# Expert rows padded to tiles of 128 slots instead of pairs of 256: 68 pairs, each half with its own expert

## The reference

```python
x = x + mamba2_layer(xn, ...) + moe(xn, router, gating, up, down)

def moe(x, router, gating, up, down):       # 8 experts, top 2, F = 256
    probs = softmax(x @ router)
    weights, indices = top_k(probs, 2)
    w = softmax(weights)
    fuse = silu(x @ gating[e]) * (x @ up[e])     # 128 -> 256, for each expert e of the token
    return sum over the two experts of w_e * (fuse @ down[e])   # 256 -> 128
```

## Time and profile before

| | |
|---|---|
| median of three runs | 825.52 us (822.66 to 828.09) |
| the profiled execution | 826.36 us, of which the span of the trace is 824.6 us |
| mean granted TensorE clock | 0.925 |
| router and top 2 | 0 to about 120 us |
| mamba2 layer | about 120 to 512 us |
| expert stage, first to last `gate_up` | 515.65 to 767.19 us |
| drain of the pipeline and last scatters | to about 783 us |
| sum and store | to 824.6 us |

### The profile page before, as it was taken

One profiled execution on the slowest core, in us unless ns is written; L12 is line 12 of the kernel. 1 busy time (PEld: TensorE's weight loads), 2 busy tenths in 40 slices (PEclk: granted clock), 3 DMA queues, 4 the chain that ended last, 5 costly groups with the idle time before them and its releaser, 6 DMA issues. The chain is left out here.

```text
span 824.6 us, 15776 instructions
## 1 busy us (share of the span) xinstructions
PE 649.1 (79%) x3781; PEld 546.2 (66%) x3783; DVE 608.1 (74%) x1486; ACT 469.9 (57%) x1030; POOL 455.4 (55%) x616
## 2 busy tenths in 40 slices
PE   0694638899889899988999897998888888889400
PEld 0694226787777787777778776787777777778300
DVE  7777999989989998999989996455555555546222
ACT  0441537678877877887767874345555555545200
POOL 3000017667777777777768785155555555555543
PEclk9999999989979998998989996899999999999855
DMA  9960100000000000000000043133323333333099
GB/s 303 260 139 0 28 1 25 23 25 25 25 21 20 28 21 24 25 25 24 21 21 28 24 133 92 40 98 95 87 87 91 95 91 91 88 93 93 10 272 338
DMA packets 72135, 62.52 MB, mean 76 GB/s; under 512 B 9544, under 2 KB 65231, under 8 KB 72112
## 3 DMA queue, kind: packets, MB, share of 16 engines
q1 hardware_dynamic: 63408, 45.19, 20.8%
q0 software_dynamic: 8704, 17.06, 6.0%
HBM read 30.73 MB, written 32.54 MB: 77 GB/s over the span
## 5 line engine op out<-in xcount | busy, mean ns | idle before, releaser
L442 POOL DMA_INDIRECT moe_d<-raw,slot_st x144 | 141.8, 984 | 131.9 <-issue 107.9
L416 POOL DMA_INDIRECT slots_d<-rows,slot_st x128 | 143.4, 1120 | 64.2 <-DVE xdt L1106 28.6
L1030 DVE SCALAR_TENSOR_TENSOR act<-raw,taps,act 128x512 f32<-128x512 f32 x192 | 163.2, 851 | 14.4 <-ACT act L511 11.1
L396 POOL TENSOR_TENSOR xde<-xdt,e_end 128x256 f32<-128x256 f32 x64 | 47.5, 742 | 113.2 <-DVE xdt L1106 111.5
L1223 DVE CAST x_hi<-bank 128x256 fp32r<-128x256 f32 x72 | 30.6, 425 | 104.4 <-PE bank L862 92.8
L855 PE MATMUL bank<-xw_hi,x_hi 128*128 x144 | 65.2, 453 | 30.5 <-DVE x_lo L1225 30.1
L881 PE MATMUL bank<-act,raw 128*128 x576 | 76.3, 276 | 0.7 <-issue 0.5
L662 ACT ACTIVATE raw<-bank 128x256 f32<-128x256 f32 x72 | 28.2, 392 | 85.4 <-remote 77.5
L772 PE MATMUL bank<-xdt,m_sb 128*128 128x64 f32 x512 | 74.1, 293 | 2.2 <-POOL xde L396 1.6
L772 PEld LDWEIGHTS bank<-xdt,m_sb 128*128 128x128 f32 x512 | 71.0, 211 | 4.3 <-issue 1.7
L881 PEld LDWEIGHTS bank<-act,raw 128*128 128x128 f32 x576 | 70.0, 192 | 1.5 <-issue 1.4
(11 more groups left out here) (234 smaller groups left out, 1727.0 us busy)
## 6 DMA issues: line engine op xcount, KB each, us to landing
slots_d<-rows SPq DMA_DIRECT2D x8, 1188.0 KB, 14.4
rows<-slots_d SPq DMA_DIRECT2D x72, 132.0 KB
act<-moe_d SPq DMA_DIRECT2D x12, 512.0 KB, 7.3
x_sb<-in_x SPq DMA_DIRECT2D x8, 512.0 KB, 6.6
act<-in_x SPq DMA_DIRECT2D x64, 64.0 KB
out<-x_sb SPq DMA_DIRECT2D x8, 512.0 KB, 7.2
moe_d<-raw,slot_st POOLq DMA_INDIRECT x144
slots_d<-rows,slot_st POOLq DMA_INDIRECT x128
```

Of the source, the lines that this page charges most:

```text
L396: nc.gpsimd.tensor_tensor(by_head(xde[:, u, :]), by_head(xdt[:, u, :]), per_head(e_end, nn), ALU.mult).then_inc(xde_done, 1)
L416: nc.gpsimd.indirect_dma_start(out=slots_d, out_offset=bass.IndirectOffsetOnAxis(ap=slot_st[:, r, c:c + 1], axis=0), in_=rows[:, r, c, :], ...
L442: nc.gpsimd.indirect_dma_start(out=moe_d, out_offset=bass.IndirectOffsetOnAxis(ap=slot_st[:, r, c:c + 1], axis=0), in_=ym[r][:, c * D:(c + ...
L1030: V.scalar_tensor_tensor(out=group_act(par)[:, t, :], in0=proj[:, t, k:k + GT], scalar=taps[:, t, k:k + 1], in1=group_act(par)[:, t, :], o ...
```

## The change

A tile of 128 slots (`TP` = 136 of them) takes the place of a pair as the unit of padding. An expert's slots begin at a multiple of 128. The pipeline still handles two tiles at a time, 68 pairs instead of 72, but the two halves of a pair can belong to different experts, so `eid` has an entry for each half and PE reads two entries in `gate_up` and two in `down`.

```diff
 PS = 2 * P
-MP = K * NT * P // PS + E
+TP = K * NT + E
+MP = TP // 2
...
-        eid = sb("eid", [1, MP], I32)
+        eid = sb("eid", [1, TP], I32)
...
-                    if not checked:
+                    if not isinstance(m, int) or TURN0 - 1 <= m < TURN1:
                         for fn in beside:
-                            fn(m - TURN0, r)
+                            fn(m - TURN0 + 1, r)
...
                 sp.dma_start(rows[:, r, :, :], slots_d[bass.ds((m * R + r) * PS, PS), :]
-                             .rearrange("(p c) v -> p c v", c=2)).then_inc(ld_slot[r], 16)
+                             .rearrange("(c p) v -> p c v", c=2)).then_inc(ld_slot[r], 16)
...
-            def expert(m, r):
-                return pe.value_load(eid[0:1, bass.ds(m * R + r, 1)], min_val=0, max_val=E - 1)
+            def expert(m, r, c):
+                return pe.value_load(eid[0:1, bass.ds((m * R + r) * 2 + c, 1)], min_val=0, max_val=E - 1)
 
             def gate_up(m, r):
-                ex = expert(m, r)
+                ex = [expert(m, r, c) for c in range(2)]
                 pe.wait_ge(xts_done, m * R + r + 1)
                 for c in range(2):
                     for a, (xs, w) in enumerate(((x_hi, gu_hi), (x_hi, gu_lo), (x_lo, gu_hi))):
                         gu = mm(bank[2 + 2 * (r % 2) + c][:, :], xs[:, r % 2, c * P:(c + 1) * P],
-                                w[:, bass.ds(ex * (2 * F), 2 * F)], start=(a == 0), stop=(a == 2))
+                                w[:, bass.ds(ex[c] * (2 * F), 2 * F)], start=(a == 0), stop=(a == 2))
...
             def down(m, r):
-                ex = expert(m, r)
+                ex = [expert(m, r, c) for c in range(2)]
...
-                               dn_sb[:, bass.ds(ex * (2 * D) + f * D, D)], start=(f == 0), stop=(f == 1))
+                               dn_sb[:, bass.ds(ex[c] * (2 * D) + f * D, D)], start=(f == 0), stop=(f == 1))
...
-            chain(V.tensor_scalar(cnt_i, incl[:, NT - 1, :], float(PS - 1), None, ALU.add))
-            chain(V.tensor_scalar(cnt_i, cnt_i, PS.bit_length() - 1, None, ALU.arith_shift_right))
+            chain(V.tensor_scalar(cnt_i, incl[:, NT - 1, :], float(P - 1), None, ALU.add))
+            chain(V.tensor_scalar(cnt_i, cnt_i, P.bit_length() - 1, None, ALU.arith_shift_right))
...
-            chain(V.tensor_scalar(base_s, base, float(PS), None, ALU.mult))
+            chain(V.tensor_scalar(base_s, base, float(P), None, ALU.mult))
```

More of the change, by code:

```diff
@@ L153, in program @@
         base_s = small[:, 928:936]
-        iota_r = small[:, 936:936 + MP].bitcast(I32)
-        iota_f = small[:, 1080:1080 + MP]
-        eid_f = small[:, 1220:1220 + MP]
+        iota_r = small[:, 936:936 + TP].bitcast(I32)
+        iota_f = small[:, 1080:1080 + TP]
+        eid_f = small[:, 1220:1220 + TP]
         tokid = small[:, 1360:1360 + NT].bitcast(I32)
@@ L236, in turn @@
                             fn(m + (r - lag) // R, (r - lag) % R)
-                    if not checked:
+                    if not isinstance(m, int) or TURN0 - 1 <= m < TURN1:
                         for fn in beside:
-                            fn(m - TURN0, r)
+                            fn(m - TURN0 + 1, r)
             lags = [lag for _, lag in stages]
-            assert (TURN1 - TURN0) * R == NT and 0 <= min(lags) and max(lags) <= R
+            assert (TURN1 - TURN0 + 1) * R == NT and 0 <= min(lags) and max(lags) <= R
             for m in range(TURN0):
@@ L383, in _ @@
             chain(pool.iota(rev_i, pattern=[[-1, E]], base=E, channel_multiplier=0))
-            chain(pool.iota(iota_r, pattern=[[1, MP]], base=0, channel_multiplier=0))
+            chain(pool.iota(iota_r, pattern=[[1, TP]], base=0, channel_multiplier=0))
             pool.wait_ge(consts, 1)
```

## The result

The changed kernel takes 869.2 us (median of six runs, 865.2 to 871.7), the kernel before 826.7 us on the same chip (median of six, 822.7 to 828.1). The ratio is 1.052, with an interval of 1.050 to 1.055: 5% slower. Another chip (D in the table of experiments) gave 865.2 against 826.8 us, 1.047 (1.043 to 1.051). The forecast was 873 us, slower.

What follows compares the result with a forecast made beforehand. PE's sequencer, nearly the bound in every second pair, was to become the bound at 4.45 us a pair: 826.4 + 46.7 + 1 = 874 us profiled, 873 us as median. The range was 842 to 902 us.

Steps and rivals of the forecast that it cites:

- The bound: Expert stage: PE's sequencer, ready after 2.75 us, is only 0.2 us from being the bound in every second pair.
- Two more reads at 0.75 us each: PE's sequencer, `gate_up` and `down`: two more reads of `eid` in each of 68 pairs add 1.5 us a pair.
- the late signal: PE's late signal to DVE in every second pair, now costing 1.15 us, costs nothing inside a 4.45 us pitch.
- Four offsets, 0.5 us: PE's sequencer: two more offsets each in `gate_up` and `down`, 0.5 us a pair together; lower bound nothing.
- The wait for `h_done` goes: In `turn_h`: the sequencer's wait of about 0.4 us vanishes with a pitch over 4 us.
- The sum: Expert stage: 2.35 + 1.5 + 0.5 and 0.1 for the branch, 4.45 us a pair; 67 intervals 298.2 us, 46.7 more.
- The rest: Outside the pitch: 0.5 us for the drain's reads and 0.5 us for the tables; slot fill, slot load, residual tiles nothing.
- Hidden reads: Rival: reads fit into the sequencer's waits in the expert stage; pitch 3.54 us, 811 us; chance 0.06.
- A cheaper sequencer: Rival: reads overlap or offsets fall into waits; pitch 3.95 us, 839 to 840 us; chance 0.13 for 835 to 856 us.
- The late signal on top: Rival: half of the pairs 1.15 us longer again, 337 us of stage, 911 us; chance 0.09 together with the clock.
- The clock: Rival: PE's idling lowers its clock; half of the pairs paying 1.5 us gives 923 us; chance 0.09 with the late signal.

Runs made afterwards that it cites:

- e1: Kernel before, 72 pairs, with each read of the table done twice, layout and offsets untouched: 852.4 us, ratio 1.035.
- e3: Changed kernel with all four reads a pair but the first half's expert for both halves, so without the four added offsets: 839.6 us, ratio 1.021.
- e8: Kernel before without GpSimd's indirect DMAs of the expert stage, input added in place of the experts' results: 776.7 us beside 785.7, 777.7 us beside 826.8.
- e4: Changed kernel with the range check taken off each read, but the check moved to each use of the value: 934.6 us, ratio 1.138.
- e6: Changed kernel with both experts packed in one entry, read once a pair and kept in a register: 774.8 us, ratio 0.987; again 815.8 us, ratio 0.988.
- e5: Changed kernel with both experts of a pair packed in one entry, two reads a pair: 789.4 us, ratio 1.005.

## Why the prediction was right, point by point

**The bound.** Right: PE's sequencer was close to its limit under a stage that seemed bound by the array and by DVE's late start. e1 shows it by itself: nothing but reads added to the kernel before, and the pitch goes from 3.54 to 3.93 us (3.95 was worked out).

**Two more reads at 0.75 us each.** Right in the mechanism and in the sum. In the pair shown, two reads take 1.5 us (649.3 to 650.8, and again 651.5 to 653.0). On the path they cost less than 1.5 us a pair, 0.4 us, because the pitch before held waiting that they fill: the wait for `h_done` and the late signal, as the prediction had it. In the same pair matmuls start while the sequencer is in a read: those of L863 at 650.17 us and of L871 at 650.38 us, beside the two reads. The reads are not hidden by that, as they don't run beside each other or beside the offsets in any row. The Trainium skill, page "Advanced Engine Details and Errata", section "Sequencer Loop", says that engine instructions are pushed into a queue and that others can be read and queued while a control instruction executes. The trace agrees with the first half, the queue; the second half no row here shows.

**Four offsets, 0.5 us.** Measured 0.45 us (4.42 less 3.97 of e3). Their lower bound had been nothing, and they were worth 30 us.

**The wait for `h_done` goes.** Right: L869 is at 649.2 and the register work of the next read begins at 649.3, where 0.6 us lay between L868 and the read the earlier trace rows.

**The sum.** 4.45 us a pair, measured 4.42 over the stage and 4.45 in the loop; 298.2 us of stage, measured 295.9. The late signal costs nothing any more, as worked out; it is in fact gone, which was not foreseen. Its cause was left open, and e8 shows that it needs the scatters. That it goes because at 4.4 us a pair the scatters, 2.6 us of GpSimd a pair, are further apart, fits e1 and e3 but was not tried by itself.

**The rest.** This is the term that was off, in its sign. The prediction added 1 us for the drain and the tables. From the last `gate_up` to the end the changed kernel takes 55.2 us where the kernel before takes 57.4, 2.2 us less. The reads of the drain do cost: PE's last matmul ends 8.0 us after the last `gate_up` instead of 6.4, 1.6 us later, for which the prediction took 0.5. (The tables cost what it took: seven instructions of 348 ns instead of 281, 0.5 us.) What it left out is that a late signal stood in the drain too. PE, ACT and GpSimd at the end of the drain, first before, then after (the last matmuls, the last copy of results, the last scatter; `remote` stands where the profile finds nobody that ended the wait):

```profile
771.37 2.19 PE L881 MATMUL bank<-act,raw 128*128 x16 [0.21 <-ACT raw L662]
775.92 0.66 ACT L662 ACTIVATE raw<-bank 128x256 f32<-128x256 f32 x2 [3.70 <-remote]
781.01 0.98 POOL L442 DMA_INDIRECT moe_d<-raw,slot_st  x1 [0.30 <-issue]
```

```profile
815.13 1.15 PE L882 MATMUL bank<-act,raw 128*128 x8 [0.82 <-ACT raw L663]
816.38 0.38 ACT L663 ACTIVATE raw<-bank 128x256 f32<-128x256 f32 x1 [1.65 <-PE bank L882]
819.43 0.98 POOL L443 DMA_INDIRECT moe_d<-raw,slot_st  x1 [0.30 <-issue]
```

Before, ACT copies 2.4 us after PE's last matmul; now 0.1 us after it. So the last scatter ends 12.1 us after the last `gate_up` and not 14.8. The stage also began 3.2 us earlier, which belongs to the execution and not to the change: in the fourteen traces it begins between 512.5 and 518.9 us. 826.4 + 44.3 - 2.2 - 3.2 = 865.3 us, the profiled execution. The medians are 42.5 us apart; 873 us was forecast and 869.2 measured.

**The rivals.** Hidden reads: excluded by e1. A cheaper sequencer: excluded by the pitch of 4.42 us and by e3, which prices the offsets at 0.45 us. The late signal on top: gone instead. The clock: 1.00 between 524 and 767 us; in e4, at 5.4 us a pair, it does fall, without a cost that shows in the pitch.

**The version that beats both.** Packed entries read once (e6) keep the four saved pairs and give back the reads: 1.2 to 1.3% under the kernel before on both kinds of chip, and 5.7% under the changed kernel on chip D (815.8 to 865.2).

## What to carry to other kernels

A sequencer has a time budget per step of its own, made of table reads, offsets, waits and branches, none of which count as busy: list them by source line for one step and compare the sum with the pitch before making more of an index dynamic. Saving 6% of the array's work lost 5% here because each half's own index cost two reads (0.75 us each) and four offsets (0.11 us each) in a step whose sequencer had, in every second pair, 0.2 us to spare. Where an index is needed twice and the sequencer is the limit, keep it in a register, and put two small indices in one entry (e6 took 774.8 us where e5, which reads it twice, took 789.4; in the kernel before on the same chip keeping alone changed next to nothing, 784.7 to 785.7, one run); and look where an assembler puts the checks before dropping their bounds.

## What the runs showed of the hardware that I had not expected

- The same program took 785.7 us on one chip and 823 to 827 us on the others. For e6, traced on both kinds, the spans differ by 41.6 us, of which 36.5 lie in the expert stage and 3.0 behind it: on the slower chips PE's completion signal of every second pair mostly comes 1.1 to 1.2 us late (30 and 32 of 72 pairs in the kernel before), on the faster one in one pair at most, in the kernels that were traced there. Without GpSimd's indirect DMAs of the expert stage the slower chip has an even pitch of 3.02 us too. A ratio measured on one chip need not hold on another: with one read a pair it was 0.987 and 0.988, but for the changed kernel it was 1.05 on the slower chips, and the estimate above says 1.10 for the faster one.
- A pitch of about 3.5 us that looked like a latency between engines was an average of 2.96 and 4.1, and with a busier sequencer the late signals became rare: at 3.93 us a pair (e1) 10 of 72 were late, at 3.97 us (e3) 3 of 68, at 4.42 us 1 of 68.
